# Two scatter-adds of expert rows: into a table that is copied out, or into the output itself

## The chip, the core and the metric

One NeuronCore of a Trainium2 chip runs the whole layer as one program. The metric is the device time of one execution in microseconds (us), lower is better. The engines are TensorE (PE in the profile, its weight loads apart as PEld), VectorE (DVE), ScalarE (ACT), GpSimd (POOL) and SyncE (SP). SP and ACT issue plain DMAs (SPq, ACTq). POOL issues the indirect ones, which take their row numbers from a column of indices.

## What is computed

A graph layer over 6250 nodes of 256 features. A normalised copy of x goes through a graph convolution over 100,000 edges and through an attention-like mixer, and both are added to x. The part that matters here is the last one, a mixture of 8 experts in which each node uses its best two:

```python
logits = xt @ Wr + br
top_p, top_idx = top_k(softmax(logits), 2)
weights = top_p / top_p.sum(-1, keepdims=True)
xe = layernorm(x) * ln_g[e] + ln_b[e]
h  = gelu(xe @ W1[e] + b1[e])          # 256 -> 1024
y  = h @ W2[e] + b2[e]                 # 1024 -> 256
x  = x + sum over the two experts of weights * y
```

## The kernel before, in words

Sizes: P is 128, N 6250 nodes, D 256, NT 49 row tiles of 128 (6272 rows, the last 22 of them padding), G 7 groups of CT = 7 row tiles, NX 8 experts, SLOTS 256 rows in an expert tile. The number of expert tiles is fixed at build time: MT = (6272 x 2 + 8 x 255) // 256 = 56, so there are 56 x 256 = 14,336 slots for 12,500 real (node, expert) pairs. A slot that no node fills gets a row number of its own at or above TRASH = 6272 (L1765 to L1768: `slot_pad` is TRASH plus a distinct number from 0 to 255). The experts follow one another in the tiles, and tiles that no expert needs come last, with padding slots only.

**Stages.** Edges first: POOL scatter-adds rows into three accumulators in DRAM (L1143), beside TensorE work for the mixer. Then the node stage (tensor_nodes, vector_nodes, scalar_nodes, sync_nodes): the sums are read back and multiplied by the first matrix, the batch norm's scale and shift are worked out on VectorE in a chain of small instructions (L1581 to L1591), ScalarE applies tanh in 26 pieces (L1796), TensorE makes the second product, VectorE adds it to X in SBUF (L1607), and the router's logits, choices and slot numbers follow. Then the expert stage, one loop over 56 tiles.

**ScalarE's order in the node stage.** scalar_nodes takes the root for the batch norm (L1785), issues four small DMAs that write zeros to the rows from TRASH on, two to xh_dram (L1789) and two to sum_dram (L1790), waits for the scale (L1792) and begins tanh. A new activation function needs a table load, which the profile shows as ACT_TABLE_LOAD under the line of the activation that follows.

**SyncE's order.** `summed(g)` waits until the seven row tiles of group g are complete in X and writes them with one DMA to sum_dram (L1849). `normed(g)` writes the normalised rows, weights and expert numbers to xh_dram (L1856). Both read in turn. sync_experts then waits for all seven writes of sum_dram (L2095) and loads the weights of each tile (L2089 to L2092).

**The expert loop.** For tile i POOL has gathered 2 x 128 rows of xh_dram by slot number (L2059). TensorE turns them (L1919), multiplies by W1 in three terms (L1934, 48 matmuls), and, behind the gelu of ScalarE (L2038) and the splits of both vector engines, by W2 (L1947, 48 matmuls). VectorE adds the bias (L2003) and multiplies by the weight (L2006) into yb, and POOL scatter-adds each half's 128 rows into sum_dram (L2077). Before the first scatter of a tile POOL waits until both scatters of the tile before have landed (L2076), because two adds to the same row must not overlap. VectorE reuses yb only when the scatters of two tiles before have landed (L2002). POOL's order in one turn of the loop is: two gathers for tile i + 2, two scatters for tile i.

**The end.** SyncE and ScalarE each wait for all 112 scatters (L2100, L2115), issue two quarters each of a copy from sum_dram to out (L2108), and wait for all four.

Of the kernel before, what the change touches and what calls it, by code (L numbers as in the profile page):

```python
# [5 lines left out]
P = 128  # L6
ALU = mybir.AluOpType
ACT = mybir.ActivationFunctionType
F32 = mybir.dt.float32
# [35 lines left out]
def gps_layer(nc, x, src, dst, ew, w_gnn1, w_gnn2, w_kv, w_qt, row_bkv, kv_ln, w_mix1, w_mix2, cols_mix,  # L45
              row_b2, w_router, row_br, w_up, w_down, cols_expert, row_be, out):
    N, D = x.shape
    E = src.shape[0]
    NX, _, H = w_up.shape
    NT = -(-N // P)  # L50
    NP_ = NT * P
    TAIL = N - (NT - 1) * P
# [8 lines left out]
    TRASH = NP_  # L61
    ACC_ROWS = NP_ + P
    MT = (NP_ * 2 + NX * (SLOTS - 1)) // SLOTS
    LISTS = MT * SLOTS // P
    DX = D + 4
    CT = 7
    G = NT // CT
# [14 lines left out]
    xnT_dram = nc.dram_tensor("xnT_dram", (P, KC, NP_), F32, kind="Internal").ap()  # L82
    at_dram = nc.dram_tensor("at_dram", (NG, P, NP_), F32, kind="Internal").ap()
    src_dram = nc.dram_tensor("src_dram", (EG * P, P), F32, kind="Internal").ap()
    sum_dram = nc.dram_tensor("sum_dram", (TRASH + 2 * P, D), F32, kind="Internal").ap()

    with ExitStack() as ctx:
        late = ctx.enter_context(ExitStack())

        def sem(name):  # L90
            return ctx.enter_context(nc.semaphore("s_" + name))
# [33 lines left out]
        zeros = fixed(512)  # L125
# [13 lines left out]
        X = node(NT, D)  # L139
# [23 lines left out]
        slot_i = small(LISTS, dtype=I32)  # L163
# [154 lines left out]
        in_turn, cost_in_turn, m, d = [], [], 0, 0  # L318
        while m < mix_steps or d < len(dense_cost):
            if d == len(dense_cost) or (m < mix_steps and m * len(dense_cost) <= d * mix_steps):  # L320
                in_turn, cost_in_turn, m = in_turn + [0], cost_in_turn + [1.5], m + 1
            else:
                in_turn, cost_in_turn, d = in_turn + [1], cost_in_turn + [dense_cost[d]], d + 1
# [4 lines left out]
        for q in range(NQ):  # L328
            due = sum(costs) * (q + 1) / (PACE * NQ)
            half, n = spent + (due - spent) / 2, 0  # L330
            while taken < len(costs) and spent + costs[taken] <= half:
                spent, taken, n = spent + costs[taken], taken + 1, n + 1
            mix_half.append(n)
            n = 0
            while taken < len(costs) and spent + costs[taken] <= due:
                spent, taken, n = spent + costs[taken], taken + 1, n + 1
# [1102 lines left out]
        s_rw, s_xtra = sem("rw"), sem("xtra")  # L1439
# [4 lines left out]
        s_sumd = sem("sumd")  # L1444
# [325 lines left out]
        def scalar_nodes(e):  # L1770
            def first_evict(c):
                lo, hi, w = chunk(c)
                for m in range(KC):
                    e.wait_ge(s_o1p, KC * c + m + 1)
                    e.activation(out1T[:, m, lo:hi], bank[4 + (2 * c + m) % 4][:, 0:w], ACT.Copy).then_inc(s_o1, 1)

            evicted = 0
            for u in range(pairs):
                for c in products[u]:
                    first_evict(c)  # L1780
                    evicted += 1
            for c in range(evicted, NCH):
                first_evict(c)
            e.wait_ge(s_once, NODE_VARIANCE)
            e.activation(bsc, bsc, ACT.Sqrt).then_inc(s_bnr, 1)  # L1785

            for half in range(2):
                rows = slice(TRASH + half * P, TRASH + (half + 1) * P)
                e.dma_start(xh_dram[rows, :], zeros[:, 0:DX]).then_inc(s_xtra, 16)  # L1789
                e.dma_start(sum_dram[rows, :], zeros[:, 0:D]).then_inc(s_xtra, 16)  # L1790

            e.wait_ge(s_once, NODE_SCALE)  # L1792
            for c in range(NCH):
                lo, hi, w = chunk(c)
                for m in range(KC):
                    k = e.activation(out1T[:, m, lo:hi], out1T[:, m, lo:hi], ACT.Tanh, bias=bbi[:, m:m + 1], scale=bsc[:, m:m + 1])  # L1796
                k.then_inc(s_tanh, 1)

            def norm_roots(g):
                a, b = g * CT, (g + 1) * CT  # L1800
                e.wait_ge(s_ve2, g + 1)
                e.activation(ve[:, a:b], mv[:, a:b, 1], ACT.Sqrt, bias=eps_col)
                e.activation(root2[:, a:b], mv[:, a:b, 1], ACT.Sqrt, bias=tiny_col, scale=1.0 + EPS).then_inc(s_root2, 1)

            norm_roots(0)
            norm_roots(1)
            for g in range(G):
                a, b = g * CT, (g + 1) * CT
                for t in group(g):
                    e.wait_ge(s_zp, t + 1)  # L1810
                    if t >= 2:
                        e.wait_ge(s_lg, t)
                    e.activation(zT[:, t % 2], bank[(3, 6, 7)[t % 3]][:, 0:2 * P].rearrange("p (k n) -> p k n", k=KC),
                                 ACT.Copy).then_inc(s_zT, 1)
                if g + 2 < G:
                    norm_roots(g + 2)
                e.wait_ge(s_sm, 2 * g + 2)
                e.activation(L[:, a:b], L[:, a:b], ACT.Exp)
                e.activation(prob[:, a:b], prob[:, a:b], ACT.Exp).then_inc(s_exp, 1)

            for t in range(NT):
                s = t % 4
                e.wait_ge(s_hot, 2 * t + 1)
                if t >= 4:
                    e.wait_ge(s_list, t - 3)
                for v, part in enumerate((token_hi, token_lo)):
                    k = e.activation(hot_hi[:, s, :, v, :], hot[:, s], ACT.Copy, scale=part[:, t:t + 1])  # L1827
                k.then_inc(s_hota, 1)
# [9 lines left out]
        def sync_nodes(e):  # L1838
            for u in range(SUM_EARLY, pairs):
                if u >= SUM_RING:  # L1840
                    e.wait_ge(s_accp, in_pair(u - SUM_RING)[-1] + 1)
                load_sums(e, u, s_accl[u % SUM_RING])
            e.wait_ge(s_once, NODE_BIAS)
            e.dma_start(brow, row_br.partition_broadcast(P)).then_inc(s_rw, 16)
            e.dma_start(Wr, w_router.rearrange("(k p) n -> p k n", p=P)).then_inc(s_rw, 16)

            def summed(g):
                e.wait_ge(s_x2, CT * (g + 1))
                e.dma_start(sum_dram[g * CT * P:(g + 1) * CT * P, :].rearrange("(t p) d -> p t d", p=P),  # L1849
                            X[:, g * CT:(g + 1) * CT, :]).then_inc(s_sumd, 16)  # L1850

            def normed(g):
                e.wait_ge(s_wgt, g + 1)
                e.wait_ge(s_xh, g + 1)
                e.wait_ge(s_idf, g + 1)
                e.dma_start(xh_dram[g * CT * P:(g + 1) * CT * P, :].rearrange("(t p) d -> p t d", p=P),  # L1856
                            xh[g % 3]).then_inc(s_xhd[g % 3], 16)

            summed(0)
            summed(1)  # L1860
            for g in range(G):
                if g + 2 < G:
                    summed(g + 2)
                if g:
                    normed(g - 1)
            normed(G - 1)
# [25 lines left out]
        yb = node(2, 2, D)  # L1892
# [6 lines left out]
        s_w1h, s_w2h, s_w1l, s_w2l = sem("w1h"), sem("w2h"), sem("w1l"), sem("w2l")  # L1899
        s_xeT, s_xf, s_xl, s_wr, s_ws = sem("xeT"), sem("xf"), sem("xl"), sem("wr"), sem("ws")  # L1900
        s_l1, s_g, s_hh, s_hl, s_l2 = sem("l1"), sem("g"), sem("hh"), sem("hl"), sem("l2")
        s_y, s_add, s_out = sem("y"), sem("add"), sem("out")
        TERMS = ((0, 0), (0, 1), (1, 0))

        def flat_part(Ws, i, half, j=None):
# [147 lines left out]
        def gpsimd_experts(e):  # L2053
            def gather(i):
                if i >= 3:
                    e.wait_ge(s_xeT, i - 2)
                    e.wait_ge(s_wr, 2 * (i - 2))
                for c in range(2):
                    e.indirect_dma_start(xe[:, i % 3, c, :], None, xh_dram,  # L2059
                                         bass.IndirectOffsetOnAxis(slot_i[:, 2 * i + c:2 * i + c + 1], 0)).then_inc(s_xe[i % 3], 16)  # L2060

            e.wait_ge(s_once, NODE_SLOTS)
            e.wait_ge(s_xtra, 64)
            landed_rows(e)
            e.wait_ge(s_sumd, 16 * G)
            e.wait_ge(s_xh, G)
            for i in range(3):
                gather(i)
            for i in range(MT):
                if 3 <= i + 2 < MT:  # L2070
                    gather(i + 2)
                for c in range(2):
                    n = 2 * i + c
                    e.wait_ge(s_y, n + 1)
                    if i and c == 0:
                        e.wait_ge(s_add, 16 * 2 * i)  # L2076
                    e.indirect_dma_start(sum_dram, bass.IndirectOffsetOnAxis(slot_i[:, n:n + 1], 0), yb[:, i % 2, c, :], None,  # L2077
                                         compute_op=ALU.add).then_inc(s_add, 16)

        def sync_experts(e):  # L2080
            def load(i):
# [10 lines left out]
                e.dma_start(W2[:, b], w_down[bass.ds(x_, 1), :, :].rearrange("a (k p) n -> p (a k) n", p=P)).then_inc(s_w2[b], 16)  # L2092

            e.wait_ge(s_once, NODE_EXPERTS)
            e.wait_ge(s_sumd, 16 * G)  # L2095
            e.wait_ge(s_xh, G)
            landed_rows(e)
            for i in range(MT):
                load(i)
            e.wait_ge(s_add, 16 * 2 * MT)  # L2100
            copy_out(e, (0, 2))
            e.wait_ge(s_out, 16 * 4)

        def copy_out(e, pieces):
            step = N * D // 4
            for i in pieces:
                o_, s_ = (a.rearrange("n d -> (n d)")[i * step:(i + 1) * step].rearrange("(a b) -> a b", a=80) for a in (out, sum_dram))
                e.dma_start(o_, s_).then_inc(s_out, 16)  # L2108

        tensor_experts(nc.tensor)  # L2110
        vector_experts(nc.vector)
        scalar_experts(nc.scalar)
        gpsimd_experts(nc.gpsimd)
        sync_experts(nc.sync)
        nc.scalar.wait_ge(s_add, 16 * 2 * MT)  # L2115
        copy_out(nc.scalar, (1, 3))
        nc.scalar.wait_ge(s_out, 16 * 4)

# [36 lines left out]
```

## Time and profile before

| | us |
|---|---|
| median of 3 runs | 2246.98 (2240.45 to 2256.11) |
| the profiled execution | 2244.61 |
| its span, first to last instruction | 2243.2 |
| mean granted TensorE clock | 0.885 of full speed |
| expert stage, first gather to last scatter's start | 1536.2 to 2217.4 |
| PE busy / DVE / ACT / POOL, share of the span | 82% / 71% / 50% / 57% |

A row of the chain of waits has a start, a length and what ran: the engine, the tile it wrote and the line. A row of the timeline has a start, a length, the engine, the line, the operation and, in brackets, the idle time before it with what ended it. A stage table gives for each stretch the busy time of every engine, the granted clock, the DMA engines' busy share and GB/s. For DMA issues, "to landing" counts from the issue's start until its semaphore has its full count. POOL's bar for an indirect DMA is the time in which it is issued, not the transfer.

### The profile page before, as it was taken

How to read it: one execution, taken by the hardware profiler on the slowest of the kernel's cores; microseconds unless marked ns; L12 is line 12 of the kernel's file. 1: busy time of each engine (PE TensorE's matmuls, PEld its weight loads, DVE VectorE, ACT ScalarE, POOL GpSimd, SP SyncE). 2: the span in 40 equal slices, each digit the busy share in tenths (PEclk: the TensorE clock that was granted, in tenths of full speed). 3: DMA queues.
4: the chain of work that ended last, by engine and by line, in shares of the span. 5: the costliest groups of instructions: out<-in, count | busy, mean ns of one | idle time of the engine just before them, and what ended most of it. 6: DMA issues, size and time to landing. Idle time of an engine off the chain costs nothing. (4 is left out here: it accounts for less than half of the span.)

```text
span 2243.2 us, 36774 instructions
## 1 busy us (share of the span) xinstructions
PE 1845.0 (82%) x10829; PEld 1543.1 (69%) x10829; DVE 1600.0 (71%) x5189; ACT 1122.8 (50%) x2255; POOL 1270.8 (57%) x811
## 2 busy tenths in 40 slices
PE   3689996778788888878886287757999999999994
PEld 1366675566566666657775146635999999999994
DVE  4666667887877877853332196777888888888883
ACT  2544453222232333332222025348888988988983
POOL 1467787788877877877777400002544544554551
PEclk7599998888888989988998598857999999999997
DMA  9978877687788888889997771343888888888885
GB/s 316 353 132 170 157 118 125 111 127 127 125 166 148 143 175 147 154 171 189 178 181 120 144 252 60 122 142 85 240 228 240 227 231 241 226 233 236 232 234 159
DMA packets 326116, 401.84 MB, mean 179 GB/s; under 512 B 34999, under 2 KB 267468, under 8 KB 325778
## 3 DMA queue, kind: packets, MB, share of 16 engines
q1 hardware_dynamic: 194048, 257.05, 36.9%
q0 software_dynamic: 103008, 103.83, 34.6%
q10 hardware_dynamic: 28850, 38.50, 5.3%
q8 instruction: 91, 1.49, 0.3%
q14 instruction: 119, 0.97, 0.2%
HBM read 251.13 MB, written 154.55 MB: 181 GB/s over the span
## 5 line engine op out<-in xcount | busy, mean ns | idle before, releaser
L1143 POOL DMA_INDIRECT acc_dram<-third x566 | 905.3, 1599 | 275.3 <-issue 143.4
L2077 POOL DMA_INDIRECT sum_dram<-node,small x112 | 195.9, 1749 | 314.2 <-DVE node L2006 297.2
L563 PE MATMUL bank<-work,third 128*128 128x256 f32 x1132 | 308.3, 417 | 45.2 <-ACT third L1097 41.6
L1947 PE MATMUL bank<-down_parts 128*128 128x256 f32 x2688 | 335.4, 284 | 0.0
L1934 PE MATMUL bank<-up_parts 128*128 128x256 f32 x2688 | 333.1, 284 | 2.3 <-DVE up_parts L1964 2.3
L1934 PEld LDWEIGHTS bank<-up_parts 128*128 128x128 f32 x2688 | 327.9, 193 | 2.7 <-DVE up_parts L1964 2.7
L1947 PEld LDWEIGHTS bank<-down_parts 128*128 128x128 f32 x2688 | 325.3, 191 | 0.0
L1097 ACT ACTIVATE third<-bank 128x512 f32<-128x512 f32 x283 | 168.3, 597 | 287.0 <-DMA acc_dram<-third 219.9
L563 PEld LDWEIGHTS bank<-work,third 128*128 128x128 f32 x1132 | 228.2, 214 | 84.2 <-ACT third L1097 44.3
L2059 POOL DMA_INDIRECT node<-xh_dram,small x112 | 138.7, 1239 | 217.4 <-DVE small L1768 183.6
L1087 ACT ACTIVATE third<-bank 128x512 f32<-128x512 f32 (+1 forms) x142 | 84.7, 597 | 342.6 <-PE bank L552 337.6
L495 PE MATMUL bank<-turned 128*128 128x245 f32 (+2 forms) x432 | 146.7, 441 | 86.3 <-DVE turned L793 83.3
L2038 ACT ACTIVATE node<-bank,node 128x256 f32<-128x256 f32 x448 | 187.9, 471 | 57.0 <-PE bank L1934 57.0
L883 DVE TENSOR_TENSOR third<-work,third 128x512 f32<-128x512 f32 (+1 forms) x142 | 96.6, 680 | 147.7 <-DMA work<-src_dram 94.5
L1991 DVE TENSOR_TENSOR down_parts<-node,down_parts 128x512 fp32r<-128x512 f32 x224 | 155.1, 693 | 65.5 <-ACT down_parts L2044 43.1
L552 PEld LDWEIGHTS bank<-third 128*128 128x128 f32 x1132 | 168.9, 220 | 16.2 <-issue 5.9
L552 PE MATMUL bank<-third 128*128 128x128 f32 x1132 | 176.4, 306 | 2.6 <-DVE third L886 2.1
L495 PEld LDWEIGHTS bank<-turned 128*128 128x128 f32 x432 | 76.9, 199 | 142.7 <-DVE turned L793 126.3
L886 DVE TENSOR_SCALAR third<-fixed,third 128x128 f32<-128x128 f32 x566 | 168.8, 384 | 0.0
L793 DVE TENSOR_TENSOR turned<-turned,bank 128x245 f32 (+2 forms) x216 | 95.8, 443 | 93.9 <-PE bank L495 82.3
L1954 DVE TENSOR_TENSOR up_parts<-turned,up_parts 128x512 fp32r<-128x512 f32 x224 | 153.2, 685 | 0.3 <-ACT up_parts L2012 0.3
L2044 ACT ACTIVATE down_parts<-node 128x512 fp32r<-128x512 f32 x224 | 141.6, 632 | 7.1
(270 smaller groups left out, 2963.2 us busy)
## 6 DMA issues: line engine op xcount, KB each, us to landing
turned<-in_w_up SPq DMA_DIRECT2D x56, 1024.0 KB, 5.9
turned<-in_w_down SPq DMA_DIRECT2D x56, 1024.0 KB, 11.0
work<-src_dram SPq DMA_DIRECT2D x141, 256.0 KB, 4.2
acc_dram<-fixed SPq DMA_DIRECT2D x15, 1280.0 KB, 10.2
work<-xn_dram SPq DMA_DIRECT2D x146, 128.0 KB, 3.0
work<-acc_dram SPq DMA_DIRECT2D x72, 256.0 KB, 4.6
at_dram<-turned ACTq DMA_DIRECT2D x48, 256.0 KB, 4.2
work<-at_dram ACTq DMA_DIRECT2D x24, 512.0 KB, 4.5
```

Source lines behind the costliest of these rows:

```text
L495: e.matmul(dense_bank(n)[:, 0:HI * s], one_lo[:, t % 4, :], one_hi[:, t % 3, 0:HI * s], start=True, stop=True).then_inc(s_ap, 1)
L552: k = e.matmul(bank[2][:, (t % QUAD) * P:(t % QUAD + 1) * P], OH[:, t % (S_QUADS * QUAD), :], S[:, t % (S_QUADS * QUAD), :], start=True, s ...
L563: k = e.matmul(bank[3 + h][:, (u - t) * D:(u - t + 1) * D], B[:, u % (2 * QUAD), :], win[:, q % 3, :], start=True, stop=True)
L886: k = e.tensor_scalar(OH[:, t % (S_QUADS * QUAD), :], iota_p, dst_rel[:, t:t + 1], w_c[:, t:t + 1], ALU.is_equal, ALU.mult)
L1097: e.activation(M[:, at:at + 2, :].rearrange("p a b -> p (a b)"), bank[3 + h][:, :], ACT.Copy).then_inc(s_row, 1)
L1143: e.indirect_dma_start(acc_dram[i], bass.IndirectOffsetOnAxis(put_i[:, t:t + 1], 0), M[:, t % (ROW_QUADS * QUAD), :], None, compute_op=ALU ...
L1934: k = e.matmul(ps, W1s[:, 2 * b + wp, q, h * P:(h + 1) * P], xTs[:, 2 * b + xp, q, :], start=(q == 0 and (wp, xp) == TERMS[0]), stop=(q == ...
L1947: k = e.matmul(bank[5 + c][:, 0:D], hTs[:, hp, h, c * P:(c + 1) * P], W2s[:, 2 * b + wp, h, :], start=(h == 0 and hp == 0 and wp == 0), st ...
L1954: e.tensor_tensor(flat_part(Ws, i, 1, j), flat_raw(W, i, j), flat_part(Ws, i, 0, j).bitcast(F32), ALU.subtract).then_inc(done, 1)
L1991: e.tensor_tensor(two[:, 1], hf[:, j % 2, :], two[:, 0].bitcast(F32), ALU.subtract).then_inc(s_hl, 1)
L2038: e.activation(hf[:, j % 2, (u % 2) * SLOTS:(u % 2 + 1) * SLOTS], bank[1 + j % 4][:, (u % 2) * SLOTS:(u % 2 + 1) * SLOTS], ACT.Gelu, bias= ...
L2077: e.indirect_dma_start(sum_dram, bass.IndirectOffsetOnAxis(slot_i[:, n:n + 1], 0), yb[:, i % 2, c, :], None, compute_op=ALU.add).then_inc( ...
```

## The change

sum_dram is gone. `summed(g)` writes the finished rows of X straight to out (the last group in two DMAs, six whole row tiles and the 106 rows of the last).
```diff
--- before.py
+++ after.py
@@ -82,7 +82,6 @@
     xnT_dram = nc.dram_tensor("xnT_dram", (P, KC, NP_), F32, kind="Internal").ap()
     at_dram = nc.dram_tensor("at_dram", (NG, P, NP_), F32, kind="Internal").ap()
     src_dram = nc.dram_tensor("src_dram", (EG * P, P), F32, kind="Internal").ap()
-    sum_dram = nc.dram_tensor("sum_dram", (TRASH + 2 * P, D), F32, kind="Internal").ap()
 
     with ExitStack() as ctx:
         late = ctx.enter_context(ExitStack())
@@ -1787,7 +1786,6 @@
             for half in range(2):
                 rows = slice(TRASH + half * P, TRASH + (half + 1) * P)
                 e.dma_start(xh_dram[rows, :], zeros[:, 0:DX]).then_inc(s_xtra, 16)
-                e.dma_start(sum_dram[rows, :], zeros[:, 0:D]).then_inc(s_xtra, 16)
 
             e.wait_ge(s_once, NODE_SCALE)
             for c in range(NCH):
@@ -1846,8 +1844,10 @@
 
             def summed(g):
                 e.wait_ge(s_x2, CT * (g + 1))
-                e.dma_start(sum_dram[g * CT * P:(g + 1) * CT * P, :].rearrange("(t p) d -> p t d", p=P),
-                            X[:, g * CT:(g + 1) * CT, :]).then_inc(s_sumd, 16)
+                a, n = g * CT, CT if g + 1 < G else CT - 1
+                e.dma_start(out[a * P:(a + n) * P, :].rearrange("(t p) d -> p t d", p=P), X[:, a:a + n, :]).then_inc(s_sumd, 16)
+                if g + 1 == G:
+                    e.dma_start(out[(NT - 1) * P:N, :], X[0:TAIL, NT - 1, :]).then_inc(s_sumd, 16)
 
             def normed(g):
                 e.wait_ge(s_wgt, g + 1)
@@ -1899,7 +1899,7 @@
         s_w1h, s_w2h, s_w1l, s_w2l = sem("w1h"), sem("w2h"), sem("w1l"), sem("w2l")
         s_xeT, s_xf, s_xl, s_wr, s_ws = sem("xeT"), sem("xf"), sem("xl"), sem("wr"), sem("ws")
         s_l1, s_g, s_hh, s_hl, s_l2 = sem("l1"), sem("g"), sem("hh"), sem("hl"), sem("l2")
-        s_y, s_add, s_out = sem("y"), sem("add"), sem("out")
+        s_y, s_add = sem("y"), sem("add")
         TERMS = ((0, 0), (0, 1), (1, 0))
 
         def flat_part(Ws, i, half, j=None):
@@ -2060,9 +2060,9 @@
                                          bass.IndirectOffsetOnAxis(slot_i[:, 2 * i + c:2 * i + c + 1], 0)).then_inc(s_xe[i % 3], 16)
 
             e.wait_ge(s_once, NODE_SLOTS)
-            e.wait_ge(s_xtra, 64)
+            e.wait_ge(s_xtra, 32)
             landed_rows(e)
-            e.wait_ge(s_sumd, 16 * G)
+            e.wait_ge(s_sumd, 16 * (G + 1))
             e.wait_ge(s_xh, G)
             for i in range(3):
                 gather(i)
@@ -2074,8 +2074,8 @@
                     e.wait_ge(s_y, n + 1)
                     if i and c == 0:
                         e.wait_ge(s_add, 16 * 2 * i)
-                    e.indirect_dma_start(sum_dram, bass.IndirectOffsetOnAxis(slot_i[:, n:n + 1], 0), yb[:, i % 2, c, :], None,
-                                         compute_op=ALU.add).then_inc(s_add, 16)
+                    e.indirect_dma_start(out, bass.IndirectOffsetOnAxis(slot_i[:, n:n + 1], 0), yb[:, i % 2, c, :], None,
+                                         bounds_check=N - 1, oob_is_err=False, compute_op=ALU.add).then_inc(s_add, 16)
 
         def sync_experts(e):
             def load(i):
@@ -2092,29 +2092,18 @@
                 e.dma_start(W2[:, b], w_down[bass.ds(x_, 1), :, :].rearrange("a (k p) n -> p (a k) n", p=P)).then_inc(s_w2[b], 16)
 
             e.wait_ge(s_once, NODE_EXPERTS)
-            e.wait_ge(s_sumd, 16 * G)
+            e.wait_ge(s_sumd, 16 * (G + 1))
             e.wait_ge(s_xh, G)
             landed_rows(e)
             for i in range(MT):
                 load(i)
             e.wait_ge(s_add, 16 * 2 * MT)
-            copy_out(e, (0, 2))
-            e.wait_ge(s_out, 16 * 4)
-
-        def copy_out(e, pieces):
-            step = N * D // 4
-            for i in pieces:
-                o_, s_ = (a.rearrange("n d -> (n d)")[i * step:(i + 1) * step].rearrange("(a b) -> a b", a=80) for a in (out, sum_dram))
-                e.dma_start(o_, s_).then_inc(s_out, 16)
 
         tensor_experts(nc.tensor)
         vector_experts(nc.vector)
         scalar_experts(nc.scalar)
         gpsimd_experts(nc.gpsimd)
         sync_experts(nc.sync)
-        nc.scalar.wait_ge(s_add, 16 * 2 * MT)
-        copy_out(nc.scalar, (1, 3))
-        nc.scalar.wait_ge(s_out, 16 * 4)
 
 
 def kernel(x, src, dst, edge_weight, L0_gnn_weight1, L0_gnn_weight2, L0_gnn_gamma, L0_gnn_beta, L0_mix_w_qkv,
```

## Rows read from the trace of the kernel before

**Rows 1.** The page, busy tenths in 40 slices of the span
```profile
PE   3689996778788888878886287757999999999994
...
POOL 1467787788877877877777400002544544554551
```

**Rows 2.** Stage table: 648 us of the expert loop, PE, PEld, DVE, ACT, POOL, clock, DMA
```profile
1560.00:2208.00 648.00, 648.00 (x5428) 648.00 (x5427) 576.71 (x1140) 583.17 (x1191) 325.05 (x216) 1.00 0.83 228
```

**Rows 3.** The chain of waits to its end
```profile
2208.62 5.77 PE bank L1947 x48
...
2215.50 1.56 POOL sum_dram L2077
...
2217.36 1.55 POOL sum_dram L2077
```

**Rows 4.** The copies at the end, line L2108: issues, and DMA to landing
```profile
L2108 ACTq DMA_DIRECT2D out<-sum_dram x2: 644/734/823, 2221.1 to 2221.8; - x2
...
DMA to landing us min/median/max: 10.0/17.3/21.4
```

**Rows 5.** Stage table: after the last scatter's issue, and from the copies' issue
```profile
2218.90:2221.10 2.20, 0.00 (x0) 0.00 (x0) 0.00 (x0) 0.00 (x0) 0.01 (x1) 0.50 0.52 60
2221.10:2243.20 22.10, 0.00 (x0) 0.00 (x0) 0.00 (x0) 0.00 (x0) 0.00 (x0) 0.50 0.89 290
```

**Rows 6.** The chain of waits, batch norm to tanh
```profile
1350.98 0.45 ACTq L1790
...
1351.45 0.48 ACTq L1789
...
1351.96 0.47 ACTq L1790
...
1352.46 1.28 ACT L1796
...
1353.76 17.80 ACT third L1796 x26
```

**Rows 7.** Timeline, ACT and DVE in the same stretch
```profile
1348.96 1.28 ACT L1785 ACT_TABLE_LOAD   x1
...
1350.38 0.17 DVE L1583 TENSOR_SCALAR work<-work 128x2 f32<-128x2 f32 x1
...
1351.41 0.16 DVE L1591 TENSOR_TENSOR work<-work,fixed 128x2 f32<-128x2 f32 x1
```

**Rows 8.** Timeline of POOL, one turn of the expert loop and the next scatter
```profile
1906.16 1.62 POOL L2077 DMA_INDIRECT sum_dram<-node,small  x1 [4.94 <-DVE node L2006]
1908.08 1.96 POOL L2077 DMA_INDIRECT sum_dram<-node,small  x1 [0.30 <-issue]
1910.34 1.41 POOL L2059 DMA_INDIRECT node<-xh_dram,small  x1 [0.30 <-issue]
1912.06 1.11 POOL L2059 DMA_INDIRECT node<-xh_dram,small  x1 [0.31 <-issue]
1918.10 1.62 POOL L2077 DMA_INDIRECT sum_dram<-node,small  x1 [4.93 <-DVE node L2006]
```

**Rows 9.** Line L2077, the scatters into sum_dram
```profile
L2077 POOL DMA_INDIRECT sum_dram<-node,small x112: 1553/1628/2001, 1560.8 to 2217.4; - x112
...
DMA to landing us min/median/max: 3.7/7.4/9.8
```

**Rows 10.** Who POOL's scatters waited for, from 1536 us on: us, times, longest
```profile
POOL sum_dram L2077 <- DVE node L2006: 297.2, 56, 16.8
```

**Rows 11.** Lines L2059 (gathers) and L1143 (scatters of the edges)
```profile
L2059 POOL DMA_INDIRECT node<-xh_dram,small x112: 949/1113/1443, 1536.2 to 2186.8; - x112
...
L1143 POOL DMA_INDIRECT acc_dram<-third x566: 1559/1561/2196, 95.7 to 1265.1; - x189
```

**Rows 12.** Timeline of SP, end of the node stage
```profile
1453.53 0.36 SPq L1849 DMA_DIRECT2D sum_dram<-node  x1
...
1492.44 0.41 SPq L2089 DMA_DIRECT2D turned<-in_w_up  x1
```

## The prediction, as it was put on record

> **What bounds the kernel now.** I read the busy slices first, to see the stages. TensorE is near full from the twenty-ninth slice on, the expert loop, and POOL is half busy there [rows 1]. The stage table confirms it: in 648 us of that loop TensorE is busy for 648, at a granted clock of 1.00, the 2.4 GHz level [rows 2]. An engine other than TensorE can cost time inside the loop only if it falls more than its own slack behind.
>
> Then the chain of waits, read from its end. It leaves TensorE with the last 48 matmuls of L1947, passes through VectorE, and ends on POOL with two scatters one behind the other, of 1.56 and 1.55 us, the second begun at 2217.36 [rows 3]. The chain's rows stop there, but the span goes on to 2243.2. The stage table of the rest shows why: no engine computes, and for 22.10 us the DMA engines are 0.89 busy [rows 5]. These are the four copies from sum_dram to out, issued from 2221.1 on, the slowest landing 21.4 us after its issue at 2221.8 [rows 4]. So the end hangs on copies, and nothing lies beside them.
>
> One more stretch matters, because the change edits it. Between the batch norm and tanh the chain runs through ScalarE's own DMA issues (L1790, L1789, L1790), then the table load, then tanh [rows 6].
>
> **The change part by part.** All sums are made against the profiled execution, 2244.61 us with a span of 2243.2. It lies 2.37 us under the median of 2246.98.
>
> Copy at the end. The last scatter lands 3.7 us (the shortest landing of L2077 [rows 9]) after 2217.36, at 2221.06, and the copies start at 2221.1. After the change the program is over when that scatter has landed. Removed: 2243.2 - 2221.1 = 22.1 us, all of it on the path [rows 5]. The Trainium skill prices this otherwise: DMA: Bandwidth & Descriptors, section Anatomy of one DMA, fits 2.0 us plus bytes over 436 GB/s to a DMA from GpSimd, which as an estimate makes 2.0 + 14.7 = 16.7 us of the 6.4 MB that are copied. With it the gain would be 5.4 us smaller. The trace disagrees, since this copy reads and writes DRAM and is four DMAs from other queues, and the row decides.
>
> Zeros for sum_dram. Two DMA issues of 0.45 and 0.47 us leave ScalarE's queue at 1350.98 and 1351.96 [rows 6], with 0.03 us to the next each: the table load would begin at 1352.46 - 0.98 = 1351.48. The other thing it could need is the batch norm's shift, complete at 1351.41 + 0.16 = 1351.57 [rows 7]. The table load for the root began at 1348.96, before the value that its activation waits for was made (1350.38 + 0.17) [rows 7], so a table load does not wait for that, and 1351.48 stands. If this one did wait, it would begin at 1351.6, 0.85 us earlier than now. The gain is 0.85 to 0.98 us at tanh, which is on the chain for 17.80 us [rows 6]; all behind it moves up. Bound against: an equal wait appears further on, and it is 0. I take 0.9, as the chain passes through both issues.
>
> summed(g). The seven writes stay, to another tensor of the same kind of memory. The last is two DMAs, one more issue of 0.36 us on SP at 1453.53; what stands on SP behind it and matters, the weight loads, begins at 1492.44 [rows 12]. The waits for s_sumd on SP and POOL are met some 35 us before anyone passes them. Cost 0; without that cover it would be 0.36. The waits for s_xtra (32 in place of 64) count two DMAs fewer and have been met for 180 us when POOL reads them. Cost 0.
>
> The bound on each scatter. No row of this trace shows an indirect DMA with a bound, so its cost x on POOL for one scatter is unknown. From below: a scatter without rows might be no work at all, x = -1.55. From above: the longest scatter of this trace is 2.196 us, 0.64 above its kind [rows 11]. The nearest row is the difference that another extra makes in the same kind of instruction: a gather of 128 rows takes 1.11 us, a scatter with the add 1.56 [rows 11], so the add costs 0.45. A comparison is less than an add with its own addresses; I take x = +0.2. In the loop it costs nothing while POOL has slack: it waits 297.2 us in 56 turns for VectorE, 5.3 us each [rows 10]. A tighter limit is the landing (L2076). From the first scatter's start to the second's is 1.92 us [rows 8], the second lands 7.4 us after its own [rows 9], and the turn takes 11.94 us (1906.16 to 1918.10 [rows 8]). That leaves 2.6 us, so x up to 1.3 is free in the loop. At the end both scatters stand on the path: 2x = +0.4 us.
>
> Padding slots. 14,336 - 12,500 = 1836 slots hold no pair. Routing the reference's own inputs gives 52 tiles that hold one, so tiles 53 to 56 are padding alone and the last two scatters have no row to move. Now the last lands 3.7 - 1.55 = 2.15 us after POOL has issued it [rows 3, 9]. Without rows that is between 0 and 2.15; nothing in the trace is nearer to either end, so I take the middle, -1.1. Less traffic in the loop is worth nothing to a TensorE that never waits [rows 2].
>
> Sum: -22.1 - 0.9 + 0.4 - 1.1 = -23.7. That is 2220.9 us against 2244.61, and 2223.3 against the median; I give 2223. The bounds: -22.1 - 0.98 - 3.1 - 2.15 = -28.3, and -22.1 + 1.3 = -20.8.
>
> **The rivals.**
>
> A, slower: the bound makes the building of a scatter long, and POOL's turn becomes the limit. The place is the loop's scatter, wait for landing, scatter. Up to x = 1.3 it is hidden. From there each of some 54 turns grows by 2x - 2.6, while the end grows by 2x. It eats the whole gain (24.1 without the check) where 54(2x - 2.6) + 2x = 24.1, at x = 1.5: scatters of 3.1 us in place of 1.63. At twice the time, x = 1.63, it is 35.6 + 3.3 - 24.1 = +14.8, 2262 us. For it: the addresses are worked out in software, row by row, and a branch for each row might slow a loop that has none. Against it: all 790 indirect DMAs lie between 0.95 and 2.2 us [rows 9, 11], whether they add or not. Chance 0.09.
>
> B, the end gives part of it back: faster, but by less than 1%. Either the check costs near 1.3 us a scatter (x free in the loop, +2.6 at the end, no gain from empty scatters: -22.1 - 0.9 + 2.6 = -20.4), or the zero writes turn out to be covered and the empty scatter lands as late as a full one (-22.1 + 0.4 = -21.7). Times 2225 to 2227. For it: nothing shows yet that a skipped row is cheaper than a written one. Chance 0.16.
>
> C, the change doesn't do what it says: a row above the bound is still carried through the queue as an empty transfer, and in the loop the adds into out land later than into sum_dram. The landing may grow by 2.6 us before POOL's turn feels it; a landing of 9.8 us, the longest now [rows 9], still fits. So this comes out as B does, unless landings pass 10 us; I count it 0.02 on the slow side, with A's time.
>
> A page bears on C. DMA: Bandwidth & Descriptors of the Trainium skill, section Anatomy of one DMA, puts most of a DMA's fixed 2.0 us down to the receipt of its last write; if an empty scatter has no receipt to wait for, as an estimate nearly all of 2.15 us would go, and the sum would be one us lower. No row shows it.
>
> **How the numbers follow.** Forecast 0.73, A 0.09, B 0.16, C 0.02. About 1%, 22.5 us here, is what a measurement of this kernel can tell from no change, and the forecast lies just beyond it. Its bounds reach to both sides of it and the three runs spread by 15.7 us, so of its 0.73 I give 0.5 to faster by over 1% and 0.23 to within. B goes to within. With A and C slower: 0.50, 0.39, 0.11. The range: the bounds make 2218.7 to 2226.2 on the median, and the runs lay 6.5 below and 9.1 above their median. A median of some runs moves by half of that, so 2214 at the low end; at the top 2236, which also takes in a check that has begun to cost in the loop. Rival A beyond it is left out.
>
> **What would show it.** The span ends within 4 us of the last scatter's start, and no DMA stretch of 22 us follows. The chain from batch norm to tanh has two DMA issues, and tanh begins near 1352.8. L2077's successor has a median of 1.7 to 2.0 us, and POOL still waits some 5 us a turn for VectorE; if it waits for its own landing instead, A is there. The last landing is under 3.7 us if empty scatters are cheap. The prediction is wrong if a turn of the loop is longer than 11.94 us, or if TensorE is idle in the 648 us.

## The result, and the profile after

Ten runs of the changed kernel have a median of 2226.6 us (2216.35 to 2239.66), ten of the kernel before 2249.69 (2240.45 to 2257.18). The ratio is 0.990 with an interval of 0.987 to 0.993: 23.1 us or 1.0% faster. The forecast was 2223 us in a range of 2214 to 2236, and -23.7 us; it holds. Whether the gain is over 1% can't be told from these runs: the ratio lies on that bound.

The two profiled executions taken alone would mislead: 2244.61 and 2234.29 us, 10.3 apart. So I read the profile after in two steps, first its end, then where the other 13 us went.

The chain of waits to its end (start, length, what ran), the changed kernel:

```profile
2221.05 5.77 PE bank L1947 x48
...
2228.45 1.55 POOL out L2077
...
2230.30 1.55 POOL out L2077
```

The last scatter begins at 2230.30 and the span ends at 2233.0, 2.7 us later. Before, the same distance was 2243.2 - 2217.36 = 25.8 us [rows 3, 5]. Nothing follows the scatter now.

The chain from the batch norm to tanh:

```profile
1353.95 0.20 ACT work L1784
1354.15 0.15 ACTq L1788
...
1354.34 0.45 ACTq L1788
...
1354.81 1.28 ACT L1794
...
1356.11 17.81 ACT third L1794 x26
```

Two DMA issues stand in ScalarE's queue where four stood [rows 6], and tanh begins 2.16 us after the root in place of 3.18 (1350.58 to 1353.76). The scatters' line (ns, shortest/median/longest), and then whom POOL waited for (us, times, longest):

```profile
L2077 POOL DMA_INDIRECT out<-node,small x112: 1554/1619/2113, 1572.8 to 2230.3; - x112
```

```profile
POOL out L2077 <- DVE node L2006: 315.1, 55, 17.6
...
POOL out L2077 <- DMA out<-node,small: 5.7, 1, 5.7
```

A scatter with a bound takes 1.62 us in the median, as one without took 1.63 [rows 9], and in 55 of 56 turns POOL still waits for VectorE [rows 10]. So the loop is untouched: 657.5 us from the first scatter to the last, 656.6 before [rows 9].

Now the other 13 us. The table walks through both executions by the starts of the same instructions. "Root" is the square root of the batch norm on ScalarE.

| stretch | before | after | difference |
|---|---|---|---|
| start to the batch norm's root | 1350.6 | 1354.0 | +3.4 |
| root to first tanh | 3.2 | 2.2 | -1.0 |
| first tanh to first gather | 182.4 | 191.3 | +8.9 |
| first gather to first scatter | 24.6 | 25.4 | +0.8 |
| first to last scatter | 656.6 | 657.5 | +0.9 |
| last scatter to the end | 25.8 | 2.7 | -23.1 |

(The sum of the rounded differences is -10.1; the spans differ by 10.2.) Two rows belong to the change, -1.0 and -23.1. The +8.9 lies in the node stage. A stage table of 60 us of it (PE, PEld, DVE, ACT, POOL busy, granted clock, DMA share, GB/s), before and then after:

```profile
1400.00:1460.00 60.00, 45.24 (x241) 39.05 (x241) 43.34 (x247) 22.33 (x49) 0.00 (x0) 0.84 0.37 124
```

```profile
1400.00:1460.00 60.00, 50.75 (x214) 43.28 (x214) 36.11 (x195) 17.63 (x39) 0.00 (x0) 0.70 0.28 93
```

TensorE was granted 0.84 of its clock in one and 0.70 in the other, and got through 241 and 214 matmuls. Whether the change does that was left to repeated profiles.

### The profile page after: what moved, and what is told of

Its sections match the earlier page's. It is cut to its first block and busy times, and to the rows that moved or that the text cites. A ratio compares the mean times of both kernels' runs of the same rounds, so it can differ in the third digit from the quotient of the medians.

```text
span 2233.0 us, 36880 instructions
## 1 busy us (share of the span) xinstructions
PE 1858.1 (83%) x10829; PEld 1552.1 (70%) x10829; DVE 1599.8 (72%) x5189; ACT 1123.0 (50%) x2255; POOL 1249.0 (56%) x811
## 3 DMA queue, kind: packets, MB, share of 16 engines
q0 software_dynamic: 103008, 101.96, 33.5%
## 5 line engine op out<-in xcount | busy, mean ns | idle before, releaser
L2077 POOL DMA_INDIRECT out<-node,small x112 | 182.3, 1627 | 338.0 <-DVE node L2006 315.1
L562 PE MATMUL bank<-work,third 128*128 128x256 f32 x1132 | 312.9, 421 | 45.6 <-ACT third L1096 40.4
L2059 POOL DMA_INDIRECT node<-xh_dram,small x112 | 130.4, 1164 | 225.2 <-DVE small L1767 191.4
## 6 DMA issues: line engine op xcount, KB each, us to landing
acc_dram<-fixed SPq DMA_DIRECT2D x15, 1280.0 KB, 10.2
```

The source lines that it names most:

```text
L562: k = e.matmul(bank[3 + h][:, (u - t) * D:(u - t + 1) * D], B[:, u % (2 * QUAD), :], win[:, q % 3, :], start=True, stop=True)
L2077: e.indirect_dma_start(out, bass.IndirectOffsetOnAxis(slot_i[:, n:n + 1], 0), yb[:, i % 2, c, :], None, bounds_check=N - 1, oob_is_err=Fal ...
```

## Experiments

**1. Take the copies alone away.** The kernel before without L2108; out stays unwritten.

```diff
             e.wait_ge(s_add, 16 * 2 * MT)
-            copy_out(e, (0, 2))
-            e.wait_ge(s_out, 16 * 4)
...
-        nc.scalar.wait_ge(s_add, 16 * 2 * MT)
-        copy_out(nc.scalar, (1, 3))
-        nc.scalar.wait_ge(s_out, 16 * 4)
```

> The kernel before without the four copies at the end (out is left unwritten); the scatters still go to sum_dram, padding rows too, and the zero writes stay. Theory: the copies were 22.1 of the 23.1 us that the change is worth, so this is 22 us faster than before, ratio 0.990; its span ends 3.7 us after the start of the last scatter. Rival (the gain comes mostly from lighter scatters or from the node stage): less than 15 us faster, 0.993 or more.

Median 2239.8 us against 2253.7, ratio 0.993 (0.989 to 0.996). The time alone is inconclusive: the interval reaches from 8.6 to 25 us of gain and the point estimate, 16.5, lies between the two theories. The trace decides for the first:

```profile
2225.53 5.77 PE bank L1947 x48
...
2232.41 1.56 POOL sum_dram L2077
...
2234.27 1.55 POOL sum_dram L2077
```

and its span:

```profile
core 0: 2237.9 us, clock 0.886
```

2237.9 - 2234.27 = 3.6 us from the last scatter to the end, in place of 25.8: the copies were 22.2 us. This execution lost time elsewhere, with 196.5 us from tanh to the first gather where the profile before has 182.4.

**2. The changed kernel again**, beside it on the same chip.

> The changed kernel once more, beside the kernel without copies on one chip. Theory: 23 to 24 us faster than before (0.9895), that is 1 to 2 us below the one without copies; the span ends 2.7 us after the last scatter's start. What the batch also shows: if the spread between runs of one kernel comes from the clock in the node stage, tanh's start and the last scatter's start differ by the same amount as the spans.

Median 2232.8 us, ratio 0.991 (0.988 to 0.994), so the gain here is nearer 0.9% than 1%. It is 7.1 us under experiment 1 in the median, where 1 to 2 were expected: the traces put 22.2 us on the copies and 1.9 on the rest of the change, the medians 13.9 and 7.1. Eleven of the twelve runs without the copies lie between 2235.4 and 2246.6 us and one at 2221.6; why so few came out low was not followed up, and the split by terms rests on the traces alone. The end is 2.7 us after the last scatter's start (2217.54 to 2220.3), the root to tanh 2.2 us. The stage from tanh to the first gather took 179.7 us here, 11.6 less than in the first profile of the very same code, and the span 12.7 less. The +8.9 of the table is thus within what one code does from one execution to the next, and can't be put down to the change.

```profile
1400.00:1460.00 60.00, 45.25 (x237) 38.97 (x236) 43.59 (x248) 22.36 (x49) 0.00 (x0) 0.82 0.36 119
```

**3. The bound alone**, put on the scatters of the kernel before.

```diff
                     e.indirect_dma_start(sum_dram, bass.IndirectOffsetOnAxis(slot_i[:, n:n + 1], 0), yb[:, i % 2, c, :], None,
-                                         compute_op=ALU.add)
+                                         bounds_check=N - 1, oob_is_err=False, compute_op=ALU.add)
```

> The kernel before with the bound on the scatters into sum_dram alone; copy and zero writes stay. Theory: the bound costs nothing on POOL (median 1.62 us, as before and after), and the last scatter, whose rows are all passed over, lands 2.7 us after its start where the kernel before took 3.73, so the copies start 1.0 us sooner after it. Rival (the early landing comes from the other target or from the missing copies): 3.7 us stays.

One execution, so its time of 2248.6 us says little. In its trace the last scatter begins at 2222.4 and the copies are issued at 2225.1, 2.7 us later in place of 3.7; the span ends at 2247.2, 24.8 us after the scatter's start in place of 25.8. Copy and target are as before, so the early landing belongs to the bound. A scatter's median is 1.618 us. What passed-over rows still cost can be seen in the DMA summary of the stretch with the last scatters (packets, MB, GB/s, sizes; then POOL's queue with its share of 16 engines), before from 2202 to 2221 us with four scatters in it, then the changed kernel from 2205 to 2233 with six:

```profile
DMA packets 579, 0.56 MB, mean 29 GB/s; under 512 B 64, under 2 KB 576, under 8 KB 576
...
q0 software_dynamic: 576, 0.52, 24.0%
```

```profile
DMA packets 868, 0.06 MB, mean 2 GB/s; under 512 B 864, under 2 KB 864, under 8 KB 864
...
q0 software_dynamic: 864, 0.01, 1.5%
```

144 packets a scatter in both (576 / 4, 864 / 6), but of under 512 B and 0.01 MB in all now. Over the whole run POOL's queue has 103,008 packets in either kernel and 103.83 against 101.96 MB, 1.87 less; 1836 rows of 1024 bytes are 1.88 MB. A passed-over row is still a packet, without the data.

**4. The zero writes back in ScalarE's queue**, to an unused tensor.

```diff
                 e.dma_start(xh_dram[rows, :], zeros[:, 0:DX]).then_inc(s_xtra, 16)
+                e.dma_start(pad_dram[half * P:(half + 1) * P, :], zeros[:, 0:D]).then_inc(s_xtra, 16)
...
-            e.wait_ge(s_xtra, 32)
+            e.wait_ge(s_xtra, 64)
```

> The changed kernel with two DMAs of zeros (128 KB each, to an unused tensor) put back at their old place in ScalarE's queue. Theory: between the batch norm's root and the first tanh the distance goes back from 2.16 us to 3.18 us, and the rest follows by 0.9 to 1.0 us. Rival (the table load waits for the batch norm's shift, so the issues are half covered): a distance of 2.9 or less.

```profile
1348.53 0.20 ACT work L1786
...
1348.92 0.45 ACTq L1791
...
1349.39 0.47 ACTq L1790
...
1349.89 0.47 ACTq L1791
...
1350.39 1.28 ACT L1797
...
1351.69 4.34 ACT third L1797 x6
```

1351.69 - 1348.53 = 3.16 us, from 2.16. The table load begins 0.03 us behind the last issue, and the batch norm's shift had been complete since 1349.51, 0.9 us before: what held the load was the queue. The 1.0 us is the two issues.

**5. The other two zero writes moved as well**, from ScalarE to SyncE, ahead of the router's bias and weights. Run in two batches.

```diff
 scalar_nodes:
-            for half in range(2):
-                rows = slice(TRASH + half * P, TRASH + (half + 1) * P)
-                e.dma_start(xh_dram[rows, :], zeros[:, 0:DX]).then_inc(s_xtra, 16)
 sync_nodes:
+            for half in range(2):
+                rows = slice(TRASH + half * P, TRASH + (half + 1) * P)
+                e.dma_start(xh_dram[rows, :], zeros[:, 0:DX]).then_inc(s_xtra, 16)
             e.wait_ge(s_once, NODE_BIAS)
             e.dma_start(brow, row_br.partition_broadcast(P)).then_inc(s_rw, 16)
```

> The changed kernel with its two remaining zero writes (to xh_dram) issued from SyncE ahead of the router's weights instead of from ScalarE. Theory: the table load then stands directly behind the root, tanh waits for the load alone and begins 1.4 us after the root's start instead of 2.16: 0.7 us off the chain, about 22 to 24 us faster than before, not to be told from the changed kernel by time alone. Rival: the shift (0.99 us after the root) or SyncE's queue is late instead and nothing moves.

> The changed kernel with its two zero writes issued from SyncE, once more, as the companion of the next. Theory: 22 to 24 us faster than before, and its profile again shows 1.4 to 1.5 us from the batch norm's root to tanh; the node stage from tanh to the first gather is about 180 or about 194 us, whichever clock the run is granted.

Tanh begins 1.52 us after the root (1341.82 to 1343.34), so 0.64 us came off the chain, where 0.7 was expected. The medians, 2228.6 and 2237.2 us with ratios 0.990 (0.986 to 0.994) and 0.993 (0.990 to 0.996), don't show it, as expected; they are 29.4 and 11.8 us under those of the kernel before, on either side of the 22 to 24 expected.

**6. Rival A's price: make POOL late in the loop.** An instruction that POOL waits for stands ahead of each scatter of the changed kernel; W is 900, then 2000 elements.

```diff
+                    e.iota(idle, [[1, W]], base=0, channel_multiplier=0, allow_small_or_imprecise_dtypes=True).then_inc(s_idle, 1)
+                    e.wait_ge(s_idle, n + 1)
                     e.indirect_dma_start(out, bass.IndirectOffsetOnAxis(slot_i[:, n:n + 1], 0), yb[:, i % 2, c, :], None,
...
```

> The changed kernel with a POOL instruction of about 1 us ahead of each of the 112 scatters, which waits for it (x about 1.0 to 1.2). Slack theory of the prediction: the landing loop is 9.3 + 2x = 11.3 to 11.7 us, under the turn of 11.94, so the loop costs nothing and the end 2x = 2.0 to 2.4 us: 0.990 x 2249 + 2 = about 2229, ratio to before 0.991. Rival (the loop has less slack, as POOL also gathers): each 0.1 us a turn would be 5.6 us; a turn over 12.0 us shows it.

> The same with about 2 us (x about 2.0 to 2.2). Landing theory: the loop scatter, wait for landing, scatter takes 9.3 + 2x = 13.3 to 13.7 us, so the turn grows from 11.94 to that, 54 turns by 1.4 to 1.8 us: +76 to +95 us, and POOL waits for its own DMA. Rival (landings shrink when POOL comes later, because they were long only for the weight loads beside them): the turn is then POOL's own work, 6.1 + 4 x 0.3 + 2x = 11.3 to 11.7 us, and it costs only the 4 to 4.4 us at the end.

The delays came out larger than meant. POOL's timeline of one turn, first with W = 900, then with 2000:

```profile
1909.29 0.88 POOL L2079 IOTA node<- 128x900 f32 x1 [2.38 <-DMA out<-node,small]
1911.00 1.96 POOL L2081 DMA_INDIRECT out<-node,small  x1 [0.83 <-POOL node L2079]
1912.39 1.48 POOL L2079 IOTA node<- 128x900 f32 x1
1914.70 1.69 POOL L2081 DMA_INDIRECT out<-node,small  x1 [0.83 <-POOL node L2079]
...
1921.32 0.88 POOL L2079 IOTA node<- 128x900 f32 x1 [1.33 <-DMA out<-node,small]
1923.03 1.88 POOL L2081 DMA_INDIRECT out<-node,small  x1 [0.83 <-POOL node L2079]
```

```profile
1888.06 1.80 POOL L2079 IOTA node<- 128x2000 f32 x1 [2.17 <-DMA out<-node,small]
1890.68 1.96 POOL L2081 DMA_INDIRECT out<-node,small  x1 [0.83 <-POOL node L2079]
1892.08 2.40 POOL L2079 IOTA node<- 128x2000 f32 x1
1895.30 1.63 POOL L2081 DMA_INDIRECT out<-node,small  x1 [0.83 <-POOL node L2079]
...
1900.02 1.81 POOL L2079 IOTA node<- 128x2000 f32 x1
...
1907.33 2.08 POOL L2081 DMA_INDIRECT out<-node,small  x1 [0.83 <-POOL node L2079]
...
1915.41 1.80 POOL L2079 IOTA node<- 128x2000 f32 x1 [3.34 <-DMA out<-node,small]
```

With W = 900 the first scatter of this turn is later by 0.88 + 0.83 - 0.30 = 1.41 us and the second follows after 3.70 us in place of 1.92, 1.78 more; in the median turn it follows after 3.49, 1.57 more, so x is 1.5 to 1.6. The loop took 658.3 us, 0.7 to 1.9 more than the 656.4 to 657.6 of the executions without a delay; the time was 2231.8 us, ratio 0.991 (0.988 to 0.994). With W = 2000 it is 2.33 and 2.70, x = 2.5, the loop took 698.2 us (some 41 more, or 0.75 a turn), and the time 2271.3 us, ratio 1.008 (1.004 to 1.011): slower than before. Neither expectation has the second size. By the landing theory the loop of W = 900 would have grown by 22 to 32 us and that of W = 2000 by 130. Its rival, POOL's own work of 6.1 + 1.2 + 2x, gives 10.5 and 12.3 us a turn: no growth, then some 20 us.

The waits on a landing do not tell the two apart (waiter, for whom, us, times, longest, in 600 us of the loop), first W = 900, then 2000:

```profile
POOL node L2079 <- DMA out<-node,small: 81.1, 42, 4.0
```

```profile
POOL node L2079 <- DMA out<-node,small: 39.2, 25, 3.3
```

POOL waits for its own landings longer and more often at W = 900, where the loop hardly grew. What differs is the chain of waits over the same 600 us:

```profile
by line: PE bank L1949 45.2%; PE bank L1936 45.1%; PE bank L1921 3.5%; DMA out<-node,small 2.3%; POOL out L2081 1.1%; DMA node<-xh_dram,small 0.9%; issue 0.8%; POOL node L2079 0.8%; POOL node L2061 0.3%; POOLq L2081 0.0%; POOLq L2059 0.0%; 
```

```profile
by line: POOL node L2079 28.9%; DMA out<-node,small 25.4%; POOL out L2081 20.9%; issue 16.9%; POOL node L2061 7.4%; POOLq L2081 0.5%; POOLq L2059 0.1%; POOLq L2078 0.1%
```

At W = 900 94% of it is TensorE: POOL's waits are hidden. At W = 2000 all of it is POOL and its landings. Of these 600 us, some 47 turns, POOL waits 39.2 for a landing and 6.7 for VectorE; the other 554, 11.7 a turn, are its own work and the gaps inside it. That nearly fills the 11.94 us of a turn, so the 0.83 us of landing wait a turn comes on top: 12.7 us.

Nor is a landing one number. In the fence above the second scatter begun at 1895.30 had landed by 1900.02, after at most 4.7 us, and the one of 1907.33 only at 1915.41, 8.1 us. The added instruction also touches VectorE: its cast of the gathered rows (L1962 before, L1964 here), on no chain here, went from 573 to 1595 ns in the mean, so the loop of W = 2000 differs in more than POOL's lateness.

**7. Does the clock in the node stage depend on TensorE's work?** On top of experiment 5, 49 matmuls of 128 columns with an unused result are added: one ahead of the second product in each of the last 35 row tiles, and one ahead of the transposes in each of the last 14 (the expectation calls this one in each of the 49 row tiles; the last 14 get both). In a third kernel each is doubled.

```diff
             def second_product(t):
...
+                if t >= 2 * CT:
+                    e.matmul(bank[t % 3][:, 256:384], ones[:, :], ones[:, :], start=True, stop=True)
                 for q in range(KC):
...
             def turn(t):
...
+                if t >= NT - 2 * CT:
+                    e.matmul(bank[(3, 6, 7)[t % 3]][:, 256:384], ones[:, :], ones[:, :], start=True, stop=True)
                 for q in range(KC):
```

> The same with one added matmul of 128 columns, whose result is not used, in each of the 49 row tiles of the node stage (about 0.25 us each on TensorE, 12 us of its work in a stage where it idles some 25 of 110 us). Theory: the node stage's 180 or 194 us depend on the granted clock between 1400 and 1460 us, 0.83 or 0.67; if the clock falls because TensorE does too little, the added work holds it up and nearly all runs come out near 180 us, 5 to 10 us faster in the median than the companion. Rival (the clock falls for another reason, or more work makes it fall): the stage keeps both lengths or gets longer by up to 12 us.

> The changed kernel once more, as the companion of the two with added matmuls. Theory: 0.990 to 0.991 of before, with most runs 10 to 15 us above the fastest.

> The kernel with one added matmul a row tile and the zero writes on SyncE, again. Theory (the added work holds the clock between 1380 and 1460 us at 0.76 or more): 6 to 12 us under the changed kernel in the median, ratio to before about 0.987. Rival (the first result was a lucky draw of runs): within 3 us of the changed kernel.

> The same with two added matmuls a row tile. Theory: TensorE is busy 16.7 of 20 us in this stage, so a second one of 0.25 us (11 a stretch of 20 us, 2.7 us) about fills it and begins to delay it: the clock holds too, but the median is 0 to 5 us above one added matmul. Rival (the clock wants still more work): 3 or more us below it.

| kernel | profiled, tanh to gather, us | median, us | ratio (interval) |
|---|---|---|---|
| zero writes on SP (5, again) | 193.1 | 2237.2 | 0.993 (0.990 to 0.996) |
| one added matmul, beside it | 186.0 | 2226.7 | 0.989 (0.984 to 0.993) |
| changed kernel, third time | 193.2 | 2236.4 | 0.991 (0.988 to 0.994) |
| one added matmul, again | 184.7 | 2226.9 | 0.989 (0.986 to 0.993) |
| two added matmuls | 197.9 | 2236.9 | 0.993 (0.990 to 0.996) |

The rows of the 60 us for the changed kernel's companion (zero writes on SP), one added matmul (its second run) and two:

```profile
1400.00:1460.00 60.00, 51.25 (x208) 43.40 (x208) 36.20 (x195) 17.62 (x39) 0.00 (x0) 0.67 0.28 93
```

```profile
1400.00:1460.00 60.00, 48.01 (x284) 43.72 (x285) 40.65 (x223) 20.07 (x47) 0.00 (x0) 0.87 0.36 120
```

```profile
1400.00:1460.00 60.00, 52.29 (x322) 46.95 (x321) 39.08 (x212) 20.39 (x44) 0.00 (x0) 0.89 0.31 103
```

With one added matmul the clock was granted at 0.87, and the median fell by 10 us in each of two batches (one of the eight runs of the second took 9713 us, which no trace explains; it moves that median by under 0.1 us). The clock does not rest on two profiles: its mean over the whole execution was 0.894 to 0.899 in the other 13 runs with one added matmul and 0.883 to 0.895 in the 22 of the two companions. So the added work raises the granted clock; by what rule, these runs don't say. The stage took 186.0 and 184.7 us, not the 180 expected, and the changed kernel had 179.7 once without any added work. With two the clock stayed at 0.89, but TensorE was busy for 52.3 of the 60 us with the added work, and the gain was gone: 10 us above one added matmul, where 0 to 5 were expected. The gain in time of one added matmul is likely, not shown: the medians agree twice, 2226.7 beside 2237.2 us for its near twin and 2226.9 beside 2236.4 for the changed kernel, but the intervals of the ratios overlap.

## Why the prediction held, point by point

- **The copies, -22.1 us:** -22.2 (experiment 1). The row gave the right size. The fit of the Trainium skill (DMA: Bandwidth & Descriptors, section Anatomy of one DMA), an estimate of 16.7 us, was 5.5 us short.
- **ScalarE's issues, -0.9:** -1.0, both issues in full (experiment 4). The argument that a table load does not wait for the value of its activation held again: in experiment 5 the load begins at 1342.04, 0.76 us before the shift is complete (1342.80), and in the changed kernel at 1354.81, 0.12 before.
- **The bound, +0.4 at the end:** 0.0. The last two scatters took 1.56 and 1.55 us, as before [rows 3]. The price taken from what the add costs was too high; both bounds were wide of it.
- **Empty scatters, -1.1:** -0.9 to -1.0 (experiment 3; also 2.7 here beside 3.6 in experiment 1), and a scatter without rows keeps its time on POOL, all its packets, and a landing of 2.7 us. Middle of two bounds, so right by luck of where it lay. The half of rival C that had passed-over rows carried through the queue is true; the loop paid nothing for it. Of its other half, later landings, the third profile of the changed kernel has a median of 7.8 us and a longest of 9.4 for 7.4 and 9.8 [rows 9], too little to be felt. With no receipt to wait for, the write receipt of the Trainium skill (DMA: Bandwidth & Descriptors, section Anatomy of one DMA) would as an estimate have taken nearly all of 2.15 us away; the traces show half, 1.0. Whether the packets without data still wait for one, they don't show.
- **Sum:** -24.1 by these terms (-22.2 - 1.0 + 0.0 - 1.0 is -24.2, the table's two rows -24.1), -23.7 forecast, -23.1 between the medians of ten runs. The terms are right by the traces; that the medians agree to half a us is luck, as the two later batches with the changed kernel gave 20.9 and 18.4 us between the medians (ratio 0.991 in both).
- **summed(g):** its extra DMA cost nothing visible; SP issued it at 1465.16 and the first weight load at 1503.81.
- **Rival B, 0.16:** its two mechanisms did not occur, though by the time alone it can't be told from the forecast: the gain is 1.0% with 0.7 to 1.3 in the interval, and 0.9% in the two later batches.
- **Rival A, 0.09:** it did not occur, and its working was wrong in two places. It took the median landing of all 112 scatters, 7.4 us [rows 9], for the second scatter of a turn, whose landing the next turn waits for. Sorted by first and second, the same trace has medians of 5.9 and 9.0 us; in the turn of [rows 8] it is 5.6 and 8.4:

```profile
DMA to landing us min/median/max: 5.6/5.6/5.6
...
DMA to landing us min/median/max: 8.4/8.4/8.4
```

  With 9.0 the slack is 1.0 us and not 2.6, and x would be free up to 0.5 only. And it took the landing for fixed: with POOL late by W = 900 it is 6.8 us in the median of the turns that waited for it. The two errors pull against each other, and neither size of slack comes out: x = 1.5 to 1.6 cost at most 1.9 us in the loop where the formula gives 22 to 32, and x = 2.5 cost 41 where it gives 130. The time of 2262 us for a doubled scatter should have been some 4 to 5 us over the forecast, as an estimate from W = 900: 0.7 to 1.9 in the loop and 2x = 3.3 at the end. The chance did not hang on that, as x was 0.
- **The signs:** the span ends 2.7 us after the last scatter's start, and TensorE was busy for 648 of 648 us (1572 to 2220). A turn of the loop took 657.5 / 55 = 11.95 us for 656.6 / 55 = 11.94. Two signs missed: the scatters' median of 1.62 us lies under the 1.7 to 2.0 said, as the bound was free, and tanh began at 1356.1 and not near 1352.8, as the root itself was 3.4 us later.

What the prediction did not see is where the spread inside one kernel comes from. It read its size off three runs and took half for a median. In the five further profiled executions with neither a delay nor an added matmul nor the writes on SyncE, the stage from tanh to the first gather took 179.7, 182.5, 193.2, 196.2 and 196.5 us, with a clock of 0.82 in the first and 0.67 in the last from 1400 to 1460 us. The stages before it vary as much: the root began at 1354.0, 1354.1 and 1359.7 us in three executions of the changed kernel, and at 1341.8 and 1356.0 in the two of experiment 5. Those two took 193.7 and 193.1 us from tanh to the first gather; their spans, 2221.3 and 2235.2, differ by what came before the root. No run here shows what moves that.

## What to carry to other kernels

A copy at the very end of a program has no cover and can be priced from the trace, here to a tenth of a microsecond; where the adds can go straight to the output, padding passed over by a bound cost nothing here. Compare two profiled executions by stretches between the same instructions before comparing their spans, since an edit worth 24 us stood beside stages that differ by 12 and 14 us between executions of one code. A slack worked out from the median of a varying time (a landing) is not a threshold: the median has to be that of the instruction that is waited for, and it moved when the waiting engine came later. And a long wait is not a cost until the chain of waits passes through it.

## What had not been expected of the hardware

- The granted clock in one stage differed between executions of the same code: 0.70 and 0.82 over the same 60 us of the changed kernel, 191.3 and 179.7 us for the stage, although tanh began within 0.2 us of the same time in both, and TensorE was busy for 17.43 us from 1380 to 1400 in either. What tips it stays open; the 49 added matmuls of experiment 7 went with 0.85 and 0.87 in two profiles.
- A row that a bound passes over is still one packet in POOL's queue, and building a scatter of 128 of them takes the same 1.55 us as one of 128 written rows.
- Landings of the same scatter varied from at most 4.7 to 8.1 us within two turns of the loop beside 2 MB of weights a turn. Between its first and its second scatter of a turn they differ in the kernel before, 5.9 and 9.0 us in the median, and the second's got shorter when POOL came later.
